# A four-layer graph network on one core: cycles of two packed groups and one scalar group, with TensorE's other work between the packed ones

## Chip, cores, metric

One Trainium2 chip, one of its cores. The metric is the device time of one execution in microseconds, the median of several runs.

## What is computed

Eight graphs (B = 8) of 2048 nodes with 128 features each and a dense 2048 x 2048 adjacency. Four layers, each with a residual and a normalisation of the rows:

```python
x = _layernorm(x + gnn0(x, adj))   # out = D^-1/2 (adj + I) D^-1/2 x, then @ W.T + b
x = _layernorm(x + attention(x))   # below
x = _layernorm(x + gnn2(x, adj))   # as layer 0 with |.| in the degrees
x = _layernorm(x + gnn3(x, adj))   # without I
```

```python
mask = jnp.where(adj > 0, 0.0, -1e22)
q, k = x @ WQ, x @ WK
h = relu(q[:, None, :, :] + k[:, :, None, :])     # 2048 x 2048 x 128 for each graph
att = softmax(einsum('bijd,d->bij', h, p) + mask)
out = att @ x
```

The attention makes the time: for each graph and each of its 2048 rows i, a relu over 128 x 2048 numbers and a product with p.

## The kernel before

The kernel writes out each engine's program by hand. The features lie on the 128 partitions. For one row i of the scores an engine makes one *row*, 128 x 2048: `relu(q + k_i)`, and TensorE multiplies it with a window of 32 columns in which one column is not zero, so that one of 32 partitions of `score` grows by it. Four rows, one in each quarter of the partitions, are a *group*; 32 groups (places g = 0 to 31) are a *block* of 128 rows i; 16 blocks are a *pass*, one graph's attention. There are 8 passes and 128 blocks, numbered here from 0; the first pass is blocks 0 to 15.

There are two kinds of groups. In a *scalar group* (kind "A") ScalarE makes the four rows in float32 (L908), and TensorE takes 16 matmuls, each in two records. In a *packed group* (kind "D") VectorE (L1088) and GpSimd (L688) make the rows as a maximum over pairs of half-precision numbers packed in a word; TensorE takes 32 matmuls, for the high and the low halves (L1247). `SCALAR_GROUPS` (L42) says which places are scalar, `makers` (L274) who makes each of the four rows: "DDPP" two by VectorE and two by GpSimd, "DPPP" one and three at the places of `THIRD_ROWS`, "AAAP" a scalar group with one row *lent* to GpSimd (`LENT_ROWS`). Rows lie in two rings, one for each kind, of two groups each (`RING = 2`): a row may be written when TensorE is done with the group two before it of the same kind (`rows_used`), and TensorE starts a group when all its rows are there (`rows_ready`).

Beside the scores of graph c+1, each pass does *side work* at fixed places: layers 2 and 3 of graph c, layer 0, queries and keys of graph c+2, each in four *steps* of one block (`BLOCK`: layer 2 in blocks 2 to 5 of the pass, layer 3 in 6 to 9, layer 0 in 10 to 13). A step on TensorE is 16 *pieces* of 128 x 512 (L1163, `PIECES_AT`), the self term (L1169), and a projection (L1181); ScalarE copies in between (`turn_layer`), VectorE sums and normalises (`SUM_AT`, `NORM_OUT_AT`), GpSimd adds the bias and takes roots. The adjacency of graph c+2 is transposed in 32 *units* of two halves, seven halves a block in the pass's blocks 0 to 8 (`SLOTS`, L1147); ScalarE copies each half out of one PSUM buffer `turn[1]` (`EVICT`, L808) and sums the unit's rows (`SUM_UNIT`, L818 and L821). Each block also does the softmax of the block before it: at place 1 VectorE reads the four banks of scores (`masked_scores`, L1040); group 0 of a block may write a bank only when it is read. Then ScalarE takes exponentials (`EXP_AT`, L880), TensorE transposes them (`TURN_AT`), ScalarE copies (`COPY_IN`, L884), TensorE multiplies (`MULTIPLY_AT`, L1224), VectorE normalises (`NORM_AT`) and makes the next mask (`MASK_AT`).

So four kinds of blocks: units only (21: blocks 0 to 8 of the first pass, 0 and 1 of the six middle ones), units and a step (42), a step only (42), and plain ones (23). In the two kinds with units, place 5 (`LEFT_OUT`) is a packed group instead of a scalar one: 11 scalar groups, and 12 in the others. An engine's program at a place is: the softmax's part, `side(c, place)`, then the group. Groups that follow each other on TensorE with no side work between them are shown by the trace as one run.

## Time and profile before

| | us |
|---|---|
| median of 3 runs (13930.92 to 13934.58) | 13932.96 |
| the profiled execution | 13921.96 |
| its span, first to last instruction | 13920.2 |
| TensorE busy | 12944.8 |
| ScalarE busy | 12465.2 |
| VectorE busy | 12353.1 |
| GpSimd busy | 11710.4 |

A chain of waits is followed back from the last instruction of a stretch, at each step to what released it. The profiled execution is 11.0 us under the median.

### The profile page before, as it was taken

How to read it: one execution, taken by the hardware profiler on the slowest of the kernel's cores; microseconds unless marked ns; L12 is line 12 of the kernel's file. 1: busy time of each engine (PE TensorE's matmuls, PEld its weight loads, DVE VectorE, ACT ScalarE, POOL GpSimd, SP SyncE). 2: the span in 40 equal slices, each digit the busy share in tenths (PEclk: the TensorE clock that was granted, in tenths of full speed). 3: DMA queues.
4: the chain of work that ended last, by engine and by line, in shares of the span. 5: the costliest groups of instructions: out<-in, count | busy, mean ns of one | idle time of the engine just before them, and what ended most of it. 6: DMA issues, size and time to landing. Idle time of an engine off the chain costs nothing.

```text
span 13920.2 us, 320252 instructions
## 1 busy us (share of the span) xinstructions
PE 12944.8 (93%) x143877; PEld 6304.3 (45%) x143877; DVE 12353.1 (89%) x8531; ACT 12465.2 (90%) x8292; POOL 11710.4 (84%) x6447
## 2 busy tenths in 40 slices
PE   7889989999899998999989999899998999999998
PEld 3444434444444444444444444444444444444443
DVE  6998998889988899888998889988899888998995
ACT  5999998899988999889998899988998889999994
POOL 4888888888888888888888888888888888888884
PEclk9999999999999999999999999999999999999999
DMA  4111112221122212222122211222112222111103
GB/s 143 52 46 48 52 57 82 86 64 48 61 82 89 61 43 65 85 88 61 38 74 82 87 57 45 68 85 84 56 45 73 82 83 62 36 47 56 43 16 110
DMA packets 752100, 918.85 MB, mean 66 GB/s; under 512 B 62608, under 2 KB 511120, under 8 KB 748688
## 3 DMA queue, kind: packets, MB, share of 16 engines
q1 hardware_dynamic: 750736, 898.36, 21.0%
q8 instruction: 1138, 18.64, 0.6%
q14 instruction: 226, 1.85, 0.0%
HBM read 705.23 MB, written 184.55 MB: 64 GB/s over the span
## 4 chain that ended last, share of the span: by engine, by line
PE 57%; ACT 18%; DVE 17%; POOL 6%; issue 2%; DMA 1%; SPq 0%; POOLq 0%; DVEq 0%; ACTq 0%
PE score L1247 42%; ACT scalar_rows L908 16%; DVE pair_rows L1088 15%; PE acc L1163 8%; POOL pair_rows L688 5%; PE turn L1134 3%; PE acc L1224 2%; PE acc L1181 1%; DVE q_pair L1016 0%; DMA piece<-adj_turned 0%; DVE gx L997 0%; PE acc L1169 0%; ACT q_pair L808 0%; PE turn L1193 0%; ACT att_turned L884 0%
## 5 line engine op out<-in xcount | busy, mean ns | idle before, releaser
L688 POOL TENSOR_SCALAR pair_rows<-q_pair,k_pair_cols 128x2050 f32<-128x2050 f32 x5628 | 11036.4, 1980 | 1855.6 <-PE score L1247 1827.5
L1088 DVE TENSOR_SCALAR pair_rows<-q_pair,k_pair_cols 128x2050 f32<-128x2050 f32 x4864 | 11076.7, 2341 | 1287.0 <-PE score L1247 1272.6
L908 ACT ACTIVATE scalar_rows<-q_f,k_cols 128x2048 f32<-128x2048 f32 x5808 | 11159.1, 2004 | 231.9 <-PE score L1247 222.0
L1247 PE MATMUL score<-pair_rows,unit_window 128*32 128x512 f16 x83936 | 5467.1, 396 | 713.7 <-DVE pair_rows L1088 560.6
L1247 PE MATMUL score<-scalar_rows,sign_window 128*32 128x512 f32 x46464 | 5424.5, 596 | 153.4 <-ACT scalar_rows L908 152.1
L1247 PEld LDWEIGHTS score<-pair_rows,unit_window 128*32 128x32 bf16 x83936 | 2873.8, 97 | 3452.7 <-issue 1043.0
L1247 PEld LDWEIGHTS score<-scalar_rows,sign_window 128*32 128x32 f32 x46464 | 1810.9, 110 | 2981.2 <-issue 2602.2
L1163 PE MATMUL acc<-piece,q_f 128*128 128x512 f32 x2944 | 1411.8, 602 | 17.0 <-DMA piece<-adj_turned 15.3
L808 ACT ACTIVATE q_pair<-turn 128x512 f32<-128x512 f32 x448 | 262.1, 585 | 765.5 <-PE turn L1134 765.5
L1163 PEld LDWEIGHTS acc<-piece,q_f 128*128 128x128 f32 x2944 | 502.6, 190 | 529.9 <-issue 469.1
L1224 PE MATMUL acc<-x,att_turned 128*128 128x128 f32 x4096 | 560.1, 280 | 0.0
L1224 PEld LDWEIGHTS acc<-x,att_turned 128*128 128x128 f32 x4096 | 505.6, 194 | 57.3 <-issue 57.3
L884 ACT ACTIVATE att_turned<-turn 128x512 f32<-128x512 f32 x512 | 301.4, 589 | 115.5 <-PE turn L1134 115.2
L1134 PEld LDWEIGHTS turn<-ident,att 128*128 128x128 f32 x2048 | 222.8, 145 | 321.4 <-issue 316.2
L1134 PE MATMUL turn<-ident,att 128*128 128x128 f32 x2048 | 347.9, 294 | 3.8 <-ACT att L880 3.1
L1040 DVE CUSTOM_DVE_ANT_0 att<-score,att 128x512 f32<-128x512 f32 x512 | 323.1, 685 | 11.7 <-PE score L1247 11.5
L1134 PE MATMUL turn<-ident,q_pair 128*128 128x128 f32 x1920 | 296.9, 279 | 27.7 <-DMA q_pair<-in_adj_dram 20.4
L1029 DVE TENSOR_SCALAR att<-att 128x2050 f32<-128x2050 f32 x128 | 291.7, 2279 | 0.0
L1134 PEld LDWEIGHTS turn<-ident,q_pair 128*128 128x128 f32 x1920 | 219.9, 142 | 122.3 <-issue 94.8
L880 ACT ACTIVATE att<-att,row_parts 128x2048 f32<-128x2048 f32 x128 | 256.4, 2003 | 12.9 <-DVE row_parts L1044 12.9
L821 ACT ACTIVATE y_turned<-q_pair 128x1024 bf16<-128x1024 f32 x224 | 237.0, 1058 | 7.1
L818 ACT ACTIVATE y_turned<-q_pair 128x1024 bf16<-128x1024 f32 x224 | 235.1, 1049 | 0.0
(101 smaller groups left out, 2664.9 us busy)
## 6 DMA issues: line engine op xcount, KB each, us to landing
piece<-adj_turned SPq DMA_DIRECT2D x1472, 256.0 KB, 2.8
q_pair<-in_adj_dram SPq DMA_DIRECT2D x240, 512.0 KB, 4.6
adj_turned<-q_pair SPq DMA_DIRECT2D x224, 512.0 KB, 4.9
att<-in_adj_dram SPq DMA_DIRECT2D x128, 820.0 KB, 4.9
att<-in_adj_dram SPq DMA_DIRECT2D x128, 204.0 KB, 5.1
q_f<-in_adj_dram SPq DMA_DIRECT2D x16, 512.0 KB, 5.5
gx<-in_x_dram SPq DMA_DIRECT2D x32, 256.0 KB, 3.9
adj_turned<-pair_rows SPq DMA_DIRECT2D x8, 1024.0 KB, 11.3
```

Of the source, the lines that this page charges most:

```text
L688: ins = pool.tensor_scalar(slot_row(n, g, u), pairs_of(c + 1), 3.0e38, k_pair_cols[:, t % 2, QUAD * u + g:QUAD * u + g + 1], ALU.min, ALU.max)
L808: nc.scalar.activation(stage(c)[:, k * BANK:(k + 1) * BANK], turn[1][:], ACT.Copy).then_inc(turn_free[1], 1)
L880: nc.scalar.activation(att, att, ACT.Exp, bias=neg_max, accum_out=row_sum).then_inc(exp_ready, 1)
L884: nc.scalar.activation(att_turned[:, cc % 2, :], turn[0][:], ACT.Copy).then_inc(turn_free[0], 1)
L908: ins = nc.scalar.activation(slot_row(n, g, u)[:, 0:N], q_of(c + 1), ACT.Relu, bias=k_cols[:, t % 2, QUAD * u + g:QUAD * u + g + 1])
L1029: nc.vector.tensor_scalar(att_wide[:, 0:N + 2], in_parts(att_wide), 0.0, NEG_INF, ALU.is_le, ALU.mult).then_inc(mask_ready, 1)
L1040: nc.vector.tensor_tensor_reduce(out=part, in0=score[:, cc, :], in1=part, scale=1.0, scalar=-3.0e38, op0=ALU.add, op1=ALU.max, accum_out=b ...
L1088: ins = nc.vector.tensor_scalar(slot_row(n, g, u), pairs_of(c + 1), k_pair_cols[:, t % 2, QUAD * u + g:QUAD * u + g + 1], None, ALU.max)
L1134: ins = nc.tensor.transpose(turn[k][:, j * P:(j + 1) * P], src(j), ident[:])
L1163: nc.tensor.matmul(acc[1][:], scaled(c)[:, i, :], turned, start=(i == 0), stop=(i == T - 1)) \
L1224: ins = nc.tensor.matmul(acc[0][:, 0:D], att_turned[:, cc % 2, j * P:(j + 1) * P], x1[:, cc * PER + j, :], start=(cc == 0 and j == 0), sto ...
L1247: ins = nc.tensor.matmul(score[QUAD * u:QUAD * (u + 1), cc, :], (unit_window if pair else sign_window)[:, QUAD - 1 - g:2 * QUAD - 1 - g], ...
```

## The change

Places are chosen anew. Scalar groups stand at every third place (2, 5, 8, ...) so that two packed groups and one scalar group follow each other; blocks with units or a step have eleven of them, plain ones twelve. Blocks of a step alone had twelve before. `PIECES_AT`, `SLOTS`, `TURN_AT` and `MULTIPLY_AT` put TensorE's side work at places 1, 4, 7, 10, ..., that is between the two packed groups, but for place 29. The steps' other places, those of the softmax and of queries and keys move with them, and GpSimd's extra rows (`THIRD_ROWS`, `LENT_ROWS`) too. On ScalarE, the exponentials and the copies of units, queries and keys go from ahead of a group's rows to the middle of them (`MID_ROW = 2`, the new function `copies`). `masked_scores` waits for the last group of the block, whatever its kind.

```diff
--- before.py
+++ after.py
@@ -38,14 +38,14 @@
     assert D == P and T % 2 == 0 and B > 2 and 2 * PER == T // 2
 
 
-    N_ACT = 12
-    SCALAR_GROUPS = [(a * GROUPS + GROUPS - 2) // N_ACT for a in range(N_ACT)]
-    LEFT_OUT = 5
+    SCALAR_GROUPS = {"steps": (2, 5, 8, 11, 14, 17, 20, 23, 26, 29, 31),
+                     "units": (2, 5, 8, 11, 14, 17, 20, 23, 26, 29, 31),
+                     "plain": (2, 5, 8, 11, 14, 17, 19, 22, 24, 27, 29, 31)}
     RING = 2
     PARTS = 5
     PART = (N + 2) // PARTS
     PITCH = PART + 2
-    assert PARTS % 2 == 1 and PART * PARTS == N + 2 and PART % 2 == 0 and LEFT_OUT in SCALAR_GROUPS
+    assert PARTS % 2 == 1 and PART * PARTS == N + 2 and PART % 2 == 0
 
     HALF = N // 2
     HALF_TILES = T // 2
@@ -57,17 +57,17 @@
 
 
     PLACES = T * GROUPS
-    SLOTS = [0, 6, 10, 14, 18, 23, 28]
-    EVICT = {0: 4, 6: 9, 10: 13, 14: 17, 18: 22, 23: 27, 28: 31}
-    SUM_UNIT = {0: 3, 6: 8, 10: 12, 14: 16, 18: 21, 23: 25, 28: 33}
+    SLOTS = [1, 4, 10, 19, 22, 25, 29]
+    EVICT = {1: 5, 4: 8, 10: 14, 19: 23, 22: 27, 25: 31, 29: 34}
+    SUM_UNIT = {1: 6, 4: 9, 10: 15, 19: 18, 22: 28, 25: 32, 29: 35}
     BLOCK = {"layer2": 2, "layer3": 6, "layer0": 10}
-    PIECES_AT = {-4: [0, 1, 2], 0: [3, 4, 5], 1: [6], 4: [7], 10: [8, 9], 14: [10], 18: [11], 23: [12, 13, 14, 15]}
-    SELF_AT, TURNED_AT, PROJECT_AT, SUM_AT, ROOT_AT, NORM_OUT_AT, STORE_AT = 18, 28, 28, 31, 33, 40, 41
-    SCALE_AT = {"layer2": [-25, -20, -15, -10], "layer3": [-5, -3, -1, 11], "layer0": [-5, -3, -1, 16]}
-    BIAS_AT, FIRST_LOAD_AT = 20, -8
-    QK = {"turn": 46, "copy": 49, "q": 50, "q_out": 54, "k": 55, "q_store": 56, "q_split": 58, "k_out": 59,
-          "q_high": 61, "k_store": 61, "q_pair_store": 62, "k_split": 76, "k_high": 78, "k_pair_store": 79}
-    X1_AT, X2_AT, X0_AT = 28, 34, 45
+    PIECES_AT = {-7: [0, 1, 2, 3], -3: [4, 5, 6, 7], 1: [8, 9], 4: [10], 7: [11], 13: [12], 16: [13], 19: [14, 15]}
+    SELF_AT, TURNED_AT, PROJECT_AT, SUM_AT, ROOT_AT, NORM_OUT_AT, STORE_AT = 16, 24, 22, 26, 28, 30, 31
+    SCALE_AT = {"layer2": [-25, -20, -15, -10], "layer3": [-8, -7, -6, 2], "layer0": [-8, -7, -6, 6]}
+    BIAS_AT, FIRST_LOAD_AT = 20, -12
+    QK = {"turn": 39, "copy": 43, "q": 42, "q_out": 46, "k": 45, "q_store": 48, "q_split": 49, "k_out": 49,
+          "q_high": 53, "k_store": 51, "q_pair_store": 54, "k_split": 56, "k_high": 60, "k_pair_store": 61}
+    X1_AT, X2_AT, X0_AT = 25, 30, 34
     DIAG_AT, DEGREE_AT, DIS_AT, KEEP_AT = 9 * GROUPS - 16, 9 * GROUPS + 8, 9 * GROUPS + 9, 11 * GROUPS + 9
 
     adj_turned = nc.dram_tensor("adj_turned", (B * STEPS * T, P, BANK), F32, kind="Internal").ap()
@@ -248,22 +248,28 @@
 
         block = ctx.enter_context(nc.Block())
 
-        TURN_AT = {6: 0, 10: 1, 14: 2, 18: 3}
-        COPY_IN = {10: 0, 13: 1, 18: 2, 23: 3}
-        MULTIPLY_AT = {10: 0, 14: 1, 18: 2, 23: 3}
-        MASK_AT, EXP_AT, NORM_AT, ATT_ROOT_AT, OUTPUT_AT = 24, 5, 27, 28, 31
-        MASK_LOAD_AT, K_LOAD_AT = 19, 21
+        TURN_AT = {4: 0, 7: 1, 10: 2, 13: 3}
+        COPY_IN = {8: 0, 11: 1, 14: 2, 17: 3}
+        MULTIPLY_AT = {7: 0, 10: 1, 13: 2, 16: 3}
+        MASK_AT, EXP_AT, NORM_AT, ATT_ROOT_AT, OUTPUT_AT = 22, 5, 20, 21, 24
+        MASK_LOAD_AT, K_LOAD_AT = 14, 21
+        MID_ROW = 2
 
         OPENING, FIRST, LAST, CLOSING = -2, -1, B - 2, B - 1
 
         MASKED_AT = (1, 1)
-        SPARE_AT = 9
-        THIN = (8, 9, 11, 12, 14)
-        THIRD_ROWS = {(True, True): (1, 25, 30), (True, False): (1, 25), (False, True): (1, 9, 25, 30), (False, False): (1, 25)}
-        LENT_ROWS = [(18, 3), (7, 3)]
+        ROOTS_BLOCK = 9
+        THIRD_ROWS = {"steps": (1, 3, 21, 25), "units": (1, 3, 21, 25), "roots": (1, 28), "plain": (1, 3, 21, 28)}
+        LENT_ROWS = [(11, 3), (23, 3)]
+
+        def sort_of(c, t):
+            if units_in(c, t) and t == ROOTS_BLOCK:
+                return "roots"
+            return "steps" if step_in(c, t) else "units" if units_in(c, t) else "plain"
 
         def kinds(c, t):
-            return ["A" if g in SCALAR_GROUPS and (g != LEFT_OUT or not units_in(c, t)) else "D" for g in range(GROUPS)]
+            groups = SCALAR_GROUPS[{"roots": "units"}.get(sort_of(c, t), sort_of(c, t))]
+            return ["A" if g in groups else "D" for g in range(GROUPS)]
 
         def units_in(c, t):
             return len(units_where(c, lambda u: slot_place(2 * u) // GROUPS == t)) > 0
@@ -273,11 +279,8 @@
 
         def makers(c, t, g):
             if kinds(c, t)[g] == "A":
-                lent = LENT_ROWS[:1 if step_in(c, t) else 2] if units_in(c, t) else []
-                return "".join("P" if (g, u) in lent else "A" for u in range(P // QUAD))
-            if units_in(c, t) and t == SPARE_AT and g in THIN:
-                return "DDDP"
-            return "DPPP" if g in THIRD_ROWS[units_in(c, t), step_in(c, t)] else "DDPP"
+                return "".join("P" if sort_of(c, t) == "units" and (g, u) in LENT_ROWS else "A" for u in range(P // QUAD))
+            return "DPPP" if g in THIRD_ROWS[sort_of(c, t)] else "DDPP"
 
         def one_of(c, *which):
             return c in which
@@ -410,7 +413,7 @@
             return c * 5 + 8
 
         def scored(n):
-            return groups_through(n - 1, SCALAR_GROUPS[-1]) + RING
+            return groups_through(n - 1, GROUPS - 1) + RING
 
         def flat(tiles):
             return tiles.rearrange("p t f -> p (t f)")
@@ -863,17 +866,19 @@
                         nc.scalar.activation(halves(pair_new(c))[:, :, 1], high(c), ACT.Copy, scale=(1.0, -1.0)[i]) \
                             .then_inc(high_written, 1)
 
-            def side(c, place):
+            def copies(c, place):
                 for k in range(2):
                     for u in units_where(c, lambda u: evict_place(2 * u + k) == place):
                         copy_unit(c, u, k)
+                queries_keys(c, place)
+
+            def side(c, place):
                 for u in units_where(c, lambda u: sum_place(u) == place):
                     sum_unit(c, u)
                 for name, s in steps_at(c, place, TURNED_AT):
                     turn_layer(c, name, s)
                 if place == DEGREE_AT and not one_of(c, LAST, CLOSING):
                     diag_sizes(c)
-                queries_keys(c, place)
 
             def exponentials(n):
                 act.wait_ge(neg_max_ready, n)
@@ -888,8 +893,6 @@
                     t, g = divmod(place, GROUPS)
                     before = t > 0 or not one_of(c, FIRST)
                     n = block_of(c, t)
-                    if before and g == EXP_AT:
-                        exponentials(n)
                     side(c, place)
                     if KINDS[n, g] == "A":
                         if first_made("A", n, g):
@@ -900,19 +903,24 @@
                                     act.wait_ge(piece_used, STEPS * T + AHEAD)
                             act.wait_ge(k_loaded[t % 2], (c + 1) * (T // 2 * 32) + (t // 2 * 32 + 32))
                         act.wait_ge(rows_used["A"], GROUP_NO[n, g] + 1)
-                        for u in range(P // QUAD):
-                            if before and u == 1 and g in COPY_IN:
+                    for u in range(P // QUAD):
+                        if u == MID_ROW:
+                            if before and g == EXP_AT:
+                                exponentials(n)
+                            if before and g in COPY_IN:
                                 copy_weights(c * T + (T + t - 1), COPY_IN[g])
-                            if MAKERS[n, g][u] != "A":
-                                continue
+                            copies(c, place)
+                        if MAKERS[n, g][u] == "A":
                             ins = nc.scalar.activation(slot_row(n, g, u)[:, 0:N], q_of(c + 1), ACT.Relu,
                                                        bias=k_cols[:, t % 2, QUAD * u + g:QUAD * u + g + 1])
+                    if KINDS[n, g] == "A":
                         ins.then_inc(rows_ready["A"], 1)
 
             for u in range(UNITS):
                 first_unit(u)
             for place in range(PLACES):
                 side(OPENING, place)
+                copies(OPENING, place)
             attention(FIRST)
             for c in range(B - 2):
                 attention(c)
@@ -922,6 +930,7 @@
                 copy_weights(B * T - 1, cc)
             for place in range(PLACES):
                 side(CLOSING, place)
+                copies(CLOSING, place)
 
 
         @block.vector
```

In the excerpts of the engines' programs, L1134, L1163, L1224, L1247 of before are L1143, L1172, L1233, L1256 of the change; on ScalarE L880, L884, L908, L808, L818, L821 are L885, L889, L914, L811, L821, L824.

TensorE, block 53 (block 5 of a middle pass, with units and a step): before, from the side work ahead of group 0 to the transposes around group 6. `x32` on pair rows is one packed group, `x64` two, `x16` on scalar rows one scalar group.

```order
L1134 MATMUL turn<-ident,q_pair 128x128 x4
L1163 MATMUL acc<-piece,q_f_0 128x512 x3
L1247 MATMUL score<-pair_rows,unit_window 32x512 x32
L1163 MATMUL acc<-piece,q_f_0 128x512
L1247 MATMUL score<-pair_rows,unit_window 32x512 x32
L1247 MATMUL score<-scalar_rows,sign_window 32x512 x16
L1247 MATMUL score<-pair_rows,unit_window 32x512 x32
L1163 MATMUL acc<-piece,q_f_0 128x512
L1247 MATMUL score<-pair_rows,unit_window 32x512 x64
L1134 MATMUL turn<-ident,att 128x128 x4
L1134 MATMUL turn<-ident,q_pair 128x128 x4
L1247 MATMUL score<-pair_rows,unit_window 32x512 x32
```

The same place of the change, from group 30 of the block before to group 4.

```order
L1256 MATMUL score<-pair_rows,unit_window 32x512 x32
L1256 MATMUL score<-scalar_rows,sign_window 32x512 x16
L1256 MATMUL score<-pair_rows,unit_window 32x512 x32
L1143 MATMUL turn<-ident,q_pair 128x128 x4
L1172 MATMUL acc<-piece,q_f_0 128x512 x2
L1256 MATMUL score<-pair_rows,unit_window 32x512 x32
L1256 MATMUL score<-scalar_rows,sign_window 32x512 x16
L1256 MATMUL score<-pair_rows,unit_window 32x512 x32
L1143 MATMUL turn<-ident,att 128x128 x4
L1143 MATMUL turn<-ident,q_pair 128x128 x4
L1172 MATMUL acc<-piece,q_f_0 128x512
L1256 MATMUL score<-pair_rows,unit_window 32x512 x32
```

Nothing stands between group 31 and group 0 any more; the side work stands after group 0 and after group 3, and the four packed groups 3 to 6 in a row are gone.

ScalarE in the same block, before: a unit's sums, group 2's rows, a unit's copy, the exponentials, group 7's rows (group 5 is packed), a sum and a copy, group 10's rows with a copy of weights after the first.

```order
L818 ACTIVATE y_turned,deg_part<-q_pair 128x1024
L821 ACTIVATE y_turned,abs_part<-q_pair 128x1024
L908 ACTIVATE scalar_rows<-q_f_1,k_cols 128x2048 x4
L808 ACTIVATE q_pair<-turn 128x512
L880 ACTIVATE att,row_parts<-att,row_parts 128x2048
L908 ACTIVATE scalar_rows<-q_f_1,k_cols 128x2048 x4
L818 ACTIVATE y_turned,deg_part<-q_pair 128x1024
L821 ACTIVATE y_turned,abs_part<-q_pair 128x1024
L808 ACTIVATE q_pair<-turn 128x512
L908 ACTIVATE scalar_rows<-q_f_1,k_cols 128x2048
L884 ACTIVATE att_turned<-turn 128x512
L908 ACTIVATE scalar_rows<-q_f_1,k_cols 128x2048 x3
```

The change: the last two rows of group 2, a sum, two rows of group 5, the exponentials and a copy, two rows of group 5 and two of group 8, two copies, two rows.

```order
L914 ACTIVATE scalar_rows<-q_f_1,k_cols 128x2048 x2
L821 ACTIVATE y_turned,deg_part<-q_pair 128x1024
L824 ACTIVATE y_turned,abs_part<-q_pair 128x1024
L914 ACTIVATE scalar_rows<-q_f_1,k_cols 128x2048 x2
L885 ACTIVATE att,row_parts<-att,row_parts 128x2048
L811 ACTIVATE q_pair<-turn 128x512
L914 ACTIVATE scalar_rows<-q_f_1,k_cols 128x2048 x4
L889 ACTIVATE att_turned<-turn 128x512
L811 ACTIVATE q_pair<-turn 128x512
L914 ACTIVATE scalar_rows<-q_f_1,k_cols 128x2048 x2
```

The exponentials and every copy now come after two of a scalar group's four rows.

## Rows read from the trace of the kernel before

**Rows 1.** The page: span, and busy time of each engine (share) xinstructions.

```profile
span 13920.2 us, 320252 instructions
...
PE 12944.8 (93%) x143877; PEld 6304.3 (45%) x143877; DVE 12353.1 (89%) x8531; ACT 12465.2 (90%) x8292; POOL 11710.4 (84%) x6447
```

**Rows 2.** Groups by line: shapes xcount | busy us, mean ns | idle before, releaser.

```profile
L1088 DVE TENSOR_SCALAR pair_rows<-q_pair,k_pair_cols 128x2050 f32<-128x2050 f32 x4864 | 11076.7, 2341 | 1287.0 <-PE score L1247 1272.6 <-DMA q_pair<-q_pair_kept 11.8
L688 POOL TENSOR_SCALAR pair_rows<-q_pair,k_pair_cols 128x2050 f32<-128x2050 f32 x5628 | 11036.4, 1980 | 1855.6 <-PE score L1247 1827.5 <-DMA q_pair<-q_pair_kept 24.9
```

**Rows 3.** Stretches of equal blocks: length, busy (x) by engine, PEclk, DMA share, GB/s.

```profile
194.00:1129.20 935.20, 808.76 (x9852) 381.90 (x9852) 873.08 (x487) 844.16 (x615) 820.80 (x433) 0.98 0.16 49
...
5293.20:5395.80 102.60, 89.09 (x1106) 41.74 (x1108) 97.20 (x56) 92.43 (x71) 92.63 (x50) 1.00 0.17 55
5395.80:5505.00 109.20, 95.76 (x1115) 44.27 (x1114) 98.11 (x60) 99.75 (x71) 94.85 (x53) 0.98 0.27 78
5505.00:6279.70 774.70, 732.38 (x8013) 366.95 (x8012) 685.62 (x486) 680.53 (x499) 656.43 (x361) 0.99 0.28 85
6279.70:6392.20 112.50, 103.86 (x1117) 51.31 (x1120) 91.54 (x67) 97.59 (x60) 99.73 (x62) 0.97 0.19 59
6392.20:6810.10 417.90, 410.60 (x4495) 206.29 (x4495) 372.80 (x272) 391.11 (x234) 359.54 (x198) 1.00 0.19 57
6810.10:7010.30 200.20, 180.82 (x2157) 82.99 (x2158) 194.38 (x119) 192.86 (x114) 168.47 (x90) 0.97 0.10 34
...
13170.30:13739.90 569.60, 526.08 (x6432) 237.65 (x6432) 549.10 (x323) 563.37 (x321) 492.63 (x263) 0.99 0.05 15
```

**Rows 4.** Chain of waits by engine and line: 5505.0 to 6279.7, then 194.0 to 1129.2.

```profile
by line: PE score L1247 53.1%; DVE pair_rows L1088 24.6%; PE acc L1163 10.3%; PE turn L1134 4.3%; PE acc L1224 3.4%; ACT scalar_rows L908 1.9%; DVE gx L997 1.0%; PE acc L1181 0.8%; PE acc L1169 0.5%; issue 0.2%; ACT y_turned L818 0.1%; ACT 
by line: ACT scalar_rows L908 53.2%; DVE pair_rows L1088 26.2%; PE score L1247 7.7%; issue 4.8%; ACT q_pair L808 2.5%; ACT y_turned L818 1.6%; PE turn L1134 1.5%; ACT att_turned L884 1.2%; ACT y_turned L821 0.8%; PE acc L1224 0.8%; ACTq L81
```

**Rows 5.** Chain of waits in block 53, in order of time: start us, us.

```profile
5839.03 18.14 DVE pair_rows L1088 x8
...
5915.13 3.44 PE acc L1163 x8
```

**Rows 6.** Timeline of TensorE, groups 1 to 4 of block 53: start us, us.

```profile
5839.97 2.02 PE L1247 MATMUL score<-pair_rows,unit_window 128*32 128x512 f16 x32
5841.79 3.64 PE L1247 MATMUL score<-scalar_rows,sign_window 128*32 128x512 f32 x32
5845.22 2.07 PE L1247 MATMUL score<-pair_rows,unit_window 128*32 128x512 f16 x32
5847.22 1.12 PE L1163 MATMUL acc<-piece,q_f 128*128 128x512 f32 x2
5848.27 2.04 PE L1247 MATMUL score<-pair_rows,unit_window 128*32 128x512 f16 x32
```

**Rows 7.** Timeline of TensorE, group 9 of block 53, and its stretch as in Rows 3.

```profile
5867.53 3.60 PE L1247 MATMUL score<-pair_rows,unit_window 128*32 128x512 f16 x32 [2.45 <-DVE pair_rows L1088]
...
5867.50:5871.10 3.60, 3.57 (x33) 1.12 (x33) 3.60 (x2) 0.00 (x0) 1.60 (x1) 0.53 0.00 0
```

**Rows 8.** Timeline of ScalarE in block 53, groups 5 to 10: start us, us [idle before].

```profile
5838.07 1.99 ACT L880 ACTIVATE att<-att,row_parts 128x2048 f32<-128x2048 f32 x1
...
5840.05 7.71 ACT L908 ACTIVATE scalar_rows<-q_f,k_cols 128x2048 f32<-128x2048 f32 x4
5847.64 1.06 ACT L818 ACTIVATE y_turned<-q_pair 128x1024 bf16<-128x1024 f32 x1
...
5857.36 0.60 ACT L808 ACTIVATE q_pair<-turn 128x512 f32<-128x512 f32 x1 [7.38 <-PE turn L1134]
```

**Rows 9.** Timeline of TensorE around the start of block 46.

```profile
5088.03 3.68 PE L1247 MATMUL score<-scalar_rows,sign_window 128*32 128x512 f32 x32
5092.99 2.39 PE L1247 MATMUL score<-pair_rows,unit_window 128*32 128x512 f16 x32 [1.28 <-DVE bank_max L1040]
5097.32 0.87 PE L1247 MATMUL score<-pair_rows,unit_window 128*32 128x512 f16 x12 [1.95 <-POOL pair_rows L688]
```

## The prediction, made before the change was run

> **What bounds the kernel now.** I read the page's busy line first. TensorE is busy 93% of the span, ScalarE 90%, VectorE 89%, GpSimd 84% [rows 1]; the clocks of the four make no clear bottleneck, and TensorE's idle 13920.2 - 12944.8 = 975 us is what any better order could win back, a little more if the clock rises with it. The groups by line show 4864 rows of VectorE and 5628 of GpSimd (and 84 lent ones), and that both wait for TensorE to free a row buffer, 1273 and 1828 us [rows 2]. So they wait for each other in turn, through rings of two groups.
>
> Next, the time by stretches of equal blocks [rows 3], where I divide by the number of blocks. In a middle pass (six of the eight) block 0 has units only and takes 102.6 us, block 1 109.2, blocks 2 to 8 (units and a step) 774.7/7 = 110.7, block 9 112.5, blocks 10 to 13 (a step) 417.9/4 = 104.5, blocks 14 and 15 100.1. The first pass has nine unit blocks of 935.2/9 = 103.9, the last pass ends with six plain ones of 569.6/6 = 94.9. In a step block TensorE is busy 410.6 of 417.9 us: it is the bound there. In the blocks of 110.7 us it is idle 42 of 775 us, and no other engine is above 98 of 110.7.
>
> The chain of waits says why [rows 4]: in blocks 2 to 8 VectorE's pair rows hold 24.6% of it and gx 1.0%, which is 198 of 774.7 us or 28.3 a block; in the first pass's unit blocks ScalarE's rows hold 53.2% and VectorE's 26.2%. Block 53 (pass 2, block 5) shows the place: one run of VectorE from 5839.03 until TensorE starts group 9 at 5867.53, for groups 3 to 9 [rows 5, 7]. Four packed groups stand in a row there (3, 4, 5, 6), and VectorE's two rows of each take 18.14/8 x 2 = 4.54 us, where TensorE needs 1.8.
>
> **Prices on TensorE**, start to start [rows 6]: a packed group 5841.79 - 5839.97 = 1.82, a scalar group 3.43, a packed group before other work 2.00, one piece between packed groups 1.05. Two matmul records of a piece cost 0.86 (3.44/8 x 2, [rows 5]). So a break in the score matmuls costs 0.18 going out and 1.05 - 0.86 = 0.19 coming back, at most 0.37; where the next group is scalar it is less. From group 1 to the start of group 9 TensorE took 27.56 us (5867.53 - 5839.97, rows 6 and [rows 7]) for work of 1.82 + 3.43 + 2.00 + 1.05 + 1.82 + 2.00 + 1.03 (two transposes with their break, like the piece) + 1.82 + 3.43 + 1.82 = 20.2: 7.3 lost. Group 9 then lasts 3.5 instead of 2.0, because the granted clock of that stretch is 0.53, so mostly the lower level of 1.2 GHz, after a pause of 2.45 us [rows 7]. That makes 8.9 a block, and 110.7 - 8.9 = 101.8 is TensorE's own work in such a block.
>
> **The change in loads.** Counted from the tables over all 128 blocks:
> - ScalarE 5808 to 5682 rows, -126 x 1.93 (7.71/4, [rows 8]) = -243 us. All of it is in step blocks, 48 to 44 rows; blocks 2 to 8 get one row more, 43 to 44.
> - VectorE 4864 to 4818, -46 x 2.27 = -104: two rows less in unit-only and plain blocks, one less in blocks 2 to 8, two more in step blocks.
> - GpSimd 5712 to 5884, +172 x 1.98 [rows 2] = +341, two rows more everywhere but in blocks 2 to 8.
> - TensorE: 42 scalar groups become packed, 42 x (1.82 - 3.43) = -68; 42 of the scalar groups no longer have a lent row, which lets them run full length, between 0 and +0.4 each, taken as +16; the breaks between score matmuls and other work rise from 1021 to 1152 in the program's order, 131 x 0.28 (between 0.19 and 0.37) = +37. Together about -15. Its own work hardly moves, so what is won must come from waits.
>
> The breaks are the one thing that speaks against the change in kind. The Trainium skill (TensorEngine Tiling (Array Packing), Key Properties) says that changing the tiling mode drains TensorE. If a drain cost a whole matmul's 0.6 us twice, the breaks would be +157 instead of +37 and 13,600; the rows show 0.37 at most.
>
> **Blocks 2 to 8, 42 of them.** The DDA cycles now cost TensorE 1.82 + 2.00 + 0.19 + 3.43 = 7.4 plus some 2.2 of other work, 9.6; VectorE needs 4 x 2.27 = 9.1 (6.8 where GpSimd makes three), GpSimd 7.9, ScalarE 7.7 plus copies. I walked VectorE through a block: rows of a packed group may start once the group two before is done, about 2.1 after that one's start. Its rows are ready 2 us early nearly everywhere, 0.4 early at group 28. At the block's start group 1 has one VectorE row only; it ends about 0.9 us before the scalar group 31 does, so the banks are being read when TensorE comes to group 0. So the 8.9 us go. What comes new:
> - The transpose of a unit at place 29 needs the buffer that ScalarE empties in the middle of group 31's rows. Those start when scalar group 26 is done, 3.7 after its start; two rows and a copy (3.85 + 0.6) make 8.1, TensorE is there after 3.43 + 1.82 + 2.00 = 7.25: 0.9 late, in every unit block.
> - The exponentials stand in the middle of group 5's rows, TensorE's first transpose of them at place 4. Group 2's rows start when scalar group 29 is done, 8.7 - 3.7 = 5.0 before group 0 starts; four rows and a copy (8.3), two rows (3.85) and the exponentials (2.0) end 9.2 after it [rows 8]. TensorE is there after 2.00 + 2.2 + 0.2 + 1.82 + 3.43 + 2.00 = 11.7. Where a sum precedes (5847.64 to 5857.36 - 7.38 = 2.3 us, [rows 8]) only 0.2 is left: 0.3 lost on average.
> - Projecting at place 22 needs a copy that ScalarE makes at 24, after group 23's rows: 0.3.
> I take 101.8 + 0.4 (no lent row) + 0.3 (one break more) + 1.5 = 104.0; 110.7 - 104.0 = 6.7, x 42 = **-281**. Ends: 0, and -8.9 x 42 = -374.
>
> **Unit-only blocks, 21.** There the busiest engine is ScalarE with 844.2/9 = 93.8, VectorE 97.0, GpSimd 91.2 in 103.9 us [rows 3]; after, VectorE 97.0 - 4.5 = 92.5, GpSimd 91.2 + 4.0 = 95.2. ScalarE waits there for transposes (7.38 us before one copy in block 53, [rows 8]); its copies now stand mid-group, a cycle or more behind the transpose. Halfway between 103.9 and 95.2: -4.4 x 9. Block 0 of a middle pass -3.1 x 6; block 1, which the DDA order helps too, -6.2 x 6, where GpSimd, 94.9 + 4, is next. Sum **-95**; ends 0 and -190.
>
> **Step blocks, 36 without block 9.** TensorE is the bound: -1.6 for the scalar group, +0.3 for the breaks. VectorE rises from 372.8/4 = 93.2 to 97.7, still under TensorE's 102.65 - 1.3 = 101.3, so the idle 7.3/4 = 1.8 stays: -1.3 x 36 = **-47**. Ends: +20 (the VectorE rows bind) and -1.3 - 1.8 each, -112.
>
> **Block 9 of the middle passes, 6.** The table "roots" asks for units and block 9, and no unit starts in block 9 (the 64th slot is the second half of one that starts in block 8). So this part does nothing: the block gets the rows of "steps", GpSimd 99.7 + 4.0 = 103.7 in 112.5. Taken as **0**; ends -20 and +25.
>
> **Plain blocks, 23.** 12 scalar groups as before; ScalarE is the bound of the last pass's (563.4/6 = 93.9 busy of 94.9): 0. Blocks 14 and 15 lose two VectorE rows and block 15 the queries' and keys' work: -2 x 15 = **-30**; ends 0 and -50.
>
> The opening and the closing (194 us before the first block, 180 after the last) keep their order: 0, within 10.
>
> Sum: -281 - 95 - 47 + 0 - 30 = **-453**. The profiled execution took 13921.96 (its span 13920.2), 11.0 under the median of the three runs; 13932.96 - 453 = 13480, so **13,480 us**, 3.3% less.
>
> **The rivals.**
> 1. *Fewer waits, but not most of them.* The rings stay two groups deep, and VectorE's 9.1 against TensorE's 9.6 leaves 0.5 us a cycle: each sum, norm or mask (2 to 4 us) on VectorE takes several cycles to make up. For it: the sums and norms did keep VectorE on the chain for 24.6% there, though TensorE had pauses to share. Half of the 453 stays: 13,706.
> 2. *The waits only move.* The VectorE run goes from groups 3 to 9 into every cycle and the time stays within 28 us, 0.2%, about what a measurement of this kernel can tell from no change.
> 3. *Slower: the start of a block.* Before, blocks with units or a step had a transpose, three pieces or both between group 31 and group 0, which hid VectorE's reading of the banks. Now nothing stands there. Block 46, which had nothing there either, shows the price: group 31 starts at 5088.03, group 0 at 5092.99, 1.5 over 3.43, then 2.5 over 1.82 until group 1 at 5097.32 [rows 9], 4.0 in all. In 105 blocks that is +424, and with VectorE late into groups 3 to 9 only half the gain comes, -227: 14,130. It decides if VectorE ends group 1's row after group 31; in block 46 GpSimd's three rows were late as well. Against it: the piece and transpose at place 1 and the single VectorE rows at groups 1 and 3.
> 4. *More than I say:* unit blocks reach their busiest engine and step blocks lose all idle time, 453 + 200 (the ends of unit-only and step blocks, 95 + 65, and 40 of blocks 2 to 8): 13,280.
>
> **How the numbers follow.** Forecast (from 13,350 to 13,620) 0.55, rival 4 0.15, rival 1 0.18, rival 2 0.04, rival 3 0.08. The ends of the terms add to -374 - 190 - 112 - 20 - 50 = -746 and +45, unlikely together. Range 13,260 to 13,740 leaves out rivals 2 and 3 and a rest. Faster 0.55 + 0.15 + 0.18 = 0.88, same 0.04, slower 0.08.
>
> **What would show it.** Blocks 2 to 8 at about 104 us, no wait of over 2 us for VectorE before group 5, 6 or 9, VectorE's share of their chain under 15%; the granted clock of these blocks near 1.00; TensorE idle about 530 us in all; a new wait of the unit transpose for ScalarE's copy, about 0.9 us in 63 blocks. Block 9 unchanged. I am wrong if group 0 starts late in most blocks, or if the chain of blocks 2 to 8 still has VectorE at a fifth.

## The result, and the profile after

13,566 us, median of four runs (13,555 to 13,572), against 13,932 for the kernel before on the same chip: ratio 0.9737, 95% interval 0.972 to 0.9754. That is -366 us where -453 was forecast. The forecast of 13,480 was 86 us too low, inside its range. In the profiled executions the span fell from 13,920.2 [rows 1] to 13,565.4, by 354.8. One of the four executions of `f3_roots_block`, below, took 28,219 us at a granted clock of 0.43 and is left out.

The page of the kernel after: the busy line, and the groups of the row makers (columns as in rows 2).

```profile
span 13565.4 us, 320252 instructions
...
PE 12859.9 (95%) x143877; PEld 6172.4 (46%) x143877; DVE 12293.0 (91%) x8485; ACT 12236.5 (90%) x8166; POOL 12073.6 (89%) x6619
...
L691 POOL TENSOR_SCALAR pair_rows<-q_pair,k_pair_cols 128x2050 f32<-128x2050 f32 x5842 | 11478.0, 1986 | 1158.8 <-PE score L1256 1123.7
L1097 DVE TENSOR_SCALAR pair_rows<-q_pair,k_pair_cols 128x2050 f32<-128x2050 f32 x4818 | 11010.7, 2341 | 953.9 <-PE score L1256 931.1
```

TensorE is idle 13,565.4 - 12,859.9 = 705 us, not 975 as before and not the 530 of the forecast. GpSimd's and VectorE's waits for a free row buffer fell from 1828 and 1273 us [rows 2] to 1124 and 931.

The stretches of equal blocks after, in the form of rows 3: the nine unit blocks of the first pass; block 0, block 1, blocks 2 to 8, block 9, blocks 10 to 13 and blocks 14 and 15 of a middle pass; the six last plain ones.

```profile
199.50:1092.50 893.00, 811.43 (x9852) 391.02 (x9852) 831.58 (x467) 845.52 (x612) 854.79 (x450) 0.99 0.17 51
5140.80:5239.70 98.90, 89.44 (x1104) 43.51 (x1097) 91.69 (x52) 94.76 (x69) 92.64 (x50) 1.00 0.22 67
5239.70:5343.00 103.30, 96.46 (x1121) 46.32 (x1121) 92.67 (x54) 95.84 (x72) 98.49 (x55) 1.00 0.26 80
5343.00:6079.60 736.60, 726.98 (x8018) 347.53 (x8017) 673.88 (x484) 692.82 (x503) 658.14 (x362) 1.00 0.30 90
...
6079.60:6190.10 110.50, 101.59 (x1120) 46.57 (x1119) 96.21 (x70) 91.80 (x59) 106.32 (x65) 1.00 0.20 60
...
6190.10:6610.70 420.60, 405.74 (x4496) 190.59 (x4493) 398.28 (x289) 364.58 (x221) 378.73 (x208) 1.00 0.18 54
6610.70:6806.80 196.10, 179.09 (x2155) 85.00 (x2157) 181.85 (x110) 192.45 (x113) 176.68 (x93) 0.98 0.10 33
...
12809.30:13380.90 571.60, 525.02 (x6432) 251.67 (x6432) 522.25 (x307) 563.75 (x321) 513.78 (x273) 0.99 0.05 14
```

Divided by the number of blocks and set against [rows 3]: unit-only 103.9 to 99.2, block 0 102.6 to 98.9, block 1 109.2 to 103.3; blocks 2 to 8 110.7 to 736.60/7 = 105.2, with TensorE idle 10 us in place of 42; block 9 112.5 to 110.5; **blocks 10 to 13 up**, 417.9 to 420.6, with VectorE busy 398 in place of 373. There TensorE's busy time fell from 410.6 to 405.7 as forecast, but its idle time rose from 7.3 to 14.9. Taken so over all 128 blocks from the starts of their groups:

| kind of block | forecast | measured |
|---|---|---|
| units and a step, 42 | -281 | -236 |
| units only, 21 | -95 | -103 |
| a step, 36 without block 9 | -47 | +23 |
| block 9 of middle passes, 6 | 0 | -10 |
| plain, 23 | -30 | -39 |
| opening and closing | 0 | +10 |
| sum | -453 | -355 |

The chain of waits by line, kernel after: blocks 2 to 8, blocks 10 to 13, block 9.

```profile
by line: PE score L1256 54.4%; ACT scalar_rows L914 13.2%; PE acc L1172 11.1%; PE turn L1143 4.7%; POOL pair_rows L691 4.0%; PE acc L1233 3.1%; DMA adj_turned<-q_pair 2.1%; issue 2.1%; ACT y_turned L824 0.9%; ACT y_turned L821 0.8%; PE acc 
...
by line: PE score L1256 42.5%; DVE pair_rows L1097 24.9%; PE acc L1172 7.1%; POOL pair_rows L691 6.5%; issue 4.9%; PE acc L1233 2.8%; PE turn L1143 2.5%; DVE q_pair L1025 1.9%; DVE q_pair L1019 1.2%; PE turn L1202 1.2%; DVE att L1038 0.9%; 
...
by line: POOL pair_rows L691 69.4%; PE score L1256 9.8%; POOL dis_new L741 7.3%; issue 4.4%; PE acc L1172 3.3%; POOL q_f L722 2.7%; POOL gx L729 1.1%; POOL rstd L670 0.9%; POOL row_parts L676 0.5%; POOL deg_sum L706 0.2%; POOL var_eps L668 
```

In blocks 2 to 8 VectorE's quarter [rows 4] is gone from the first places; a quarter of VectorE now stands in blocks 10 to 13 instead, and GpSimd holds block 9.

### The profile page after: what moved, and what is told of

Same layout as the page of the kernel before. It is cut to its first block, busy times and chain, and to the rows that moved or that the text cites. A ratio compares the mean times of both kernels' runs of the same rounds, so it can differ in the third digit from the quotient of the medians.

```text
span 13565.4 us, 320252 instructions
## 1 busy us (share of the span) xinstructions
PE 12859.9 (95%) x143877; PEld 6172.4 (46%) x143877; DVE 12293.0 (91%) x8485; ACT 12236.5 (90%) x8166; POOL 12073.6 (89%) x6619
## 4 chain that ended last, share of the span: by engine, by line
PE 53%; ACT 19%; POOL 14%; DVE 9%; issue 3%; DMA 1%; SPq 0%; POOLq 0%; ACTq 0%; DVEq 0%
PE score L1256 39%; ACT scalar_rows L914 16%; POOL pair_rows L691 12%; PE acc L1172 7%; DVE pair_rows L1097 7%; PE turn L1143 3%; PE acc L1233 2%; DVE q_pair L1025 1%; ACT att L885 1%; DMA adj_turned<-q_pair 1%; ACT y_turned L824 1%; ACT q_pair L811 1%; ACT y_turned L821 1%; POOL dis_new L741 0%; DMA piece<-adj_turned 0%
## 5 line engine op out<-in xcount | busy, mean ns | idle before, releaser
L691 POOL TENSOR_SCALAR pair_rows<-q_pair,k_pair_cols 128x2050 f32<-128x2050 f32 x5842 | 11478.0, 1986 | 1158.8 <-PE score L1256 1123.7
L914 ACT ACTIVATE scalar_rows<-q_f,k_cols 128x2048 f32<-128x2048 f32 x5682 | 10941.8, 2001 | 997.6 <-PE score L1256 989.2
L1256 PE MATMUL score<-pair_rows,unit_window 128*32 128x512 f16 x85280 | 5567.6, 394 | 474.2 <-POOL pair_rows L691 278.2
L1256 PE MATMUL score<-scalar_rows,sign_window 128*32 128x512 f32 x45456 | 5251.1, 595 | 81.7 <-ACT scalar_rows L914 80.2
L1256 PEld LDWEIGHTS score<-pair_rows,unit_window 128*32 128x32 bf16 x85280 | 2779.8, 96 | 3489.6 <-issue 1603.9
L1256 PEld LDWEIGHTS score<-scalar_rows,sign_window 128*32 128x32 f32 x45456 | 1784.9, 110 | 2748.5 <-issue 2350.0
L1172 PE MATMUL acc<-piece,q_f 128*128 128x512 f32 x2944 | 1408.8, 601 | 19.7 <-DMA piece<-adj_turned 18.6
L1172 PEld LDWEIGHTS acc<-piece,q_f 128*128 128x128 f32 x2944 | 504.4, 191 | 495.9 <-issue 433.0
L1233 PE MATMUL acc<-x,att_turned 128*128 128x128 f32 x4096 | 554.9, 279 | 0.0
L1233 PEld LDWEIGHTS acc<-x,att_turned 128*128 128x128 f32 x4096 | 498.4, 192 | 57.4 <-issue 57.4
L1143 PE MATMUL turn<-ident,att 128*128 128x128 f32 x2048 | 337.3, 287 | 30.3 <-ACT att_turned L889 21.7
L1143 PE MATMUL turn<-ident,q_pair 128*128 128x128 f32 x1920 | 306.8, 284 | 34.9 <-ACT q_pair L811 24.5
L1143 PEld LDWEIGHTS turn<-ident,att 128*128 128x128 f32 x2048 | 215.8, 141 | 264.4 <-issue 190.1
L889 ACT ACTIVATE att_turned<-turn 128x512 f32<-128x512 f32 x512 | 298.2, 582 | 5.3 <-PE turn L1143 5.3
L1143 PEld LDWEIGHTS turn<-ident,q_pair 128*128 128x128 f32 x1920 | 208.9, 141 | 191.9 <-issue 154.8
L811 ACT ACTIVATE q_pair<-turn 128x512 f32<-128x512 f32 x448 | 261.2, 583 | 31.0 <-DMA adj_turned<-q_pair 29.4
L885 ACT ACTIVATE att<-att,row_parts 128x2048 f32<-128x2048 f32 x128 | 255.4, 1995 | 6.4 <-DVE row_parts L1053 6.4
L824 ACT ACTIVATE y_turned<-q_pair 128x1024 bf16<-128x1024 f32 x224 | 237.2, 1059 | 7.1
L821 ACT ACTIVATE y_turned<-q_pair 128x1024 bf16<-128x1024 f32 x224 | 235.6, 1052 | 0.0
```

Source lines behind the costliest of these rows:

```text
L691: ins = pool.tensor_scalar(slot_row(n, g, u), pairs_of(c + 1), 3.0e38, k_pair_cols[:, t % 2, QUAD * u + g:QUAD * u + g + 1], ALU.min, ALU.max)
L811: nc.scalar.activation(stage(c)[:, k * BANK:(k + 1) * BANK], turn[1][:], ACT.Copy).then_inc(turn_free[1], 1)
L821: nc.scalar.activation(unread, raw(c), ACT.Copy, accum_out=deg_part[:, u % 2, u // 2:u // 2 + 1]).then_inc(raw_summed, 1)
L824: nc.scalar.activation(unread, raw(c), ACT.Abs, accum_out=abs_part[:, u % 2, u // 2:u // 2 + 1]).then_inc(raw_abs_summed, 1)
L885: nc.scalar.activation(att, att, ACT.Exp, bias=neg_max, accum_out=row_sum).then_inc(exp_ready, 1)
L914: ins = nc.scalar.activation(slot_row(n, g, u)[:, 0:N], q_of(c + 1), ACT.Relu, bias=k_cols[:, t % 2, QUAD * u + g:QUAD * u + g + 1])
```

## Experiments

### Either half alone

`e1_groups_alone` is the kernel before with the tables of groups (and the copies of weights also in packed groups); `e2_places_alone` is the change with those tables put back, so the new order within ScalarE's groups belongs to its half.

```diff
-    N_ACT = 12
-    SCALAR_GROUPS = [(a * GROUPS + GROUPS - 2) // N_ACT for a in range(N_ACT)]
+    SCALAR_GROUPS = {"steps": (2, 5, 8, 11, 14, 17, 20, 23, 26, 29, 31),
...
+        THIRD_ROWS = {"steps": (1, 3, 21, 25), "units": (1, 3, 21, 25), "roots": (1, 28), "plain": (1, 3, 21, 28)}
+        LENT_ROWS = [(11, 3), (23, 3)]
```

> The kernel before with the new scalar groups, makers and lent rows alone; all side work, softmax places and copies stand as before (where a copy of weights stood inside a scalar group that is now packed, it is made at the same place ahead of the next rows). Theory G (the groups make the gain: four packed groups in a row are gone, so VectorE no longer holds TensorE): blocks 2 to 8 of a middle pass fall from 110.7 to 106 or less, the whole to 13,650-13,750 us. Rival P (the place of the side work makes it: between two packed groups it gives VectorE its time): blocks 2 to 8 stay over 108.5, the whole at 13,800-13,930 us.

> The changed kernel with the old scalar groups, makers and lent rows: four packed groups 3 to 6 in a row in blocks with units, side work at the new places 1, 4, 7, 10, ... Theory G: VectorE's run over groups 3 to 9 stays, blocks 2 to 8 at 109-111 us, the whole at 13,830-13,950 us. Rival P: blocks 2 to 8 at 106 or less, the whole at 13,650-13,750 us. If both this and the groups alone stay over 13,800, it takes both together.

Groups alone: 13,992, ratio 1.0044 (1.0029 to 1.0059). Places alone: 13,950, ratio 1.0015 (1.0005 to 1.0025). So neither part brings the gain, and each alone costs something; together they bring 2.6%. Both theories missed the time of the first; the second came out as theory G had it (109 to 111 a block). Blocks 2 to 8 of the two, as in rows 3, and for the second the wait that is left there (us in total, times, longest):

```profile
5534.20:6286.90 752.70, 726.47 (x8013) 365.68 (x8012) 669.47 (x477) 694.86 (x506) 657.75 (x361) 1.00 0.29 87
```

```profile
5493.10:6256.90 763.80, 730.18 (x8018) 345.30 (x8013) 687.31 (x491) 682.16 (x496) 656.92 (x362) 1.00 0.29 87
...
PE score L1254 <- DVE pair_rows L1095: 27.7, 21, 2.5
```

107.5 and 109.1 a block: more than half of the 110.7 - 105.2 comes from the groups there. What the first loses is in its step blocks: blocks 12 and 13 of this pass take 111 or more each. That the extra GpSimd rows at 21 and 25 meet norms and splits at their old places there is the likely reason; no run separates it.

### Order within ScalarE, and the twelfth scalar group

`e3_copies_ahead`: `MID_ROW = 2` becomes `0`, so exponentials and copies come ahead of the four rows. `e4_twelve_in_steps`: blocks with a step and no unit keep twelve scalar groups.

> The changed kernel with MID_ROW = 0: exponentials and all copies stand ahead of a group's rows again, two rows earlier on ScalarE. Theory M (mid-group copies matter since ScalarE would otherwise wait for TensorE's transposes before it can make rows): unit-only blocks rise from 99.2 to 101-103 us and the whole to 13,610-13,680 us. Rival N (they do not matter; earlier copies even end the wait of the transpose at place 29 for its buffer, 0.55 us in 63 blocks): 13,520-13,570 us.

> The changed kernel with twelve scalar groups again in blocks that have a step and no unit (places and makers of plain blocks): VectorE 36 instead of 38 rows there, GpSimd 44 instead of 46, ScalarE 48 instead of 44. Theory V (step blocks did not gain because VectorE and GpSimd got two rows more each, beside the queries' and keys' splits): blocks 10 to 13 of a middle pass fall from 105.2 to 102-104 us, block 9 from 110.8 to 108 or less, the whole to 13,490-13,550 us. Rival T (TensorE is their bound, as forecast, and a scalar group costs it 1.6 more): blocks 10 to 13 rise to 106-107, the whole to 13,590-13,640 us.

Copies ahead: 13,691, 0.9831 (0.9817 to 0.9846), 124 us of the gain given back, more than either theory had. Blocks 2 to 8 take 756.8/7 = 108.1, and 2.9 x 42 = 122 is nearly all of it; unit-only ones did not rise to 101 as theory M had it. ScalarE in block 53 shows how, then TensorE there:

```profile
5717.20 7.70 ACT L914 ACTIVATE scalar_rows<-q_f,k_cols 128x2048 f32<-128x2048 f32 x4
5724.78 0.59 ACT L889 ACTIVATE att_turned<-turn 128x512 f32<-128x512 f32 x1
5726.61 0.60 ACT L811 ACTIVATE q_pair<-turn 128x512 f32<-128x512 f32 x1 [1.23 <-DMA adj_turned<-q_pair]
...
5721.84 2.05 PE L1256 MATMUL score<-pair_rows,unit_window 128*32 128x512 f16 x32
5724.95 3.65 PE L1256 MATMUL score<-scalar_rows,sign_window 128*32 128x512 f32 x32 [1.05 <-ACT scalar_rows L914]
```

The four rows of group 5 come behind the exponentials and a copy, and TensorE starts 3.1 after the group ahead instead of 1.8; the next copy waits for the store of the one before, and the next group's rows wait behind it.

Twelve in steps: 13,593, 0.976 (0.9745 to 0.9774). Blocks 10 to 13 take 106.9 on average, 1.7 more, about what a scalar group costs over a packed one (rival T), so eleven are right there. Block 9 takes 107.5 with it, 3 us less: that block has too much for GpSimd.

### What holds blocks 11 to 13

In a middle pass only the blocks behind a step of layer 0 got longer: block 10 went from 103.6 to 102.5, as forecast, but 11 and 12 from 105.6 to 106.4 and 13 from 103.1 to 105.3. They make the queries and keys. A *split* is two instructions of VectorE on 128x512, a bitwise and (L1019) and a subtraction (L1025). The split of q stands at place 17, that of k at place 24. VectorE in block 59 (block 11) after, then GpSimd at the one of q and, from 6359.80, at the one of k:

```profile
6342.14 0.41 DVE L1019 TENSOR_SCALAR q_pair<-q_pair 128x512 int32<-128x512 int32 x1
6342.59 0.75 DVE L1025 TENSOR_TENSOR q_pair<-q_pair 128x512 f16<-128x512 f32 x1
6343.22 9.11 DVE L1097 TENSOR_SCALAR pair_rows<-q_pair,k_pair_cols 128x2050 f32<-128x2050 f32 x4
...
6362.53 1.47 DVE L1019 TENSOR_SCALAR q_pair<-q_pair 128x512 int32<-128x512 int32 x1
6364.04 2.45 DVE L1025 TENSOR_TENSOR q_pair<-q_pair 128x512 f16<-128x512 f32 x1
6366.38 6.84 DVE L1097 TENSOR_SCALAR pair_rows<-q_pair,k_pair_cols 128x2050 f32<-128x2050 f32 x3
...
6337.68 3.92 POOL L691 TENSOR_SCALAR pair_rows<-q_pair,k_pair_cols 128x2050 f32<-128x2050 f32 x2 [1.23 <-PE score L1256]
6342.96 4.14 POOL L691 TENSOR_SCALAR pair_rows<-q_pair,k_pair_cols 128x2050 f32<-128x2050 f32 x2 [1.35 <-PE score L1256]
...
6359.80 18.26 POOL L691 TENSOR_SCALAR pair_rows<-q_pair,k_pair_cols 128x2050 f32<-128x2050 f32 x9
```

The same two instructions take 0.41 + 0.75 us where GpSimd is idle (6341.6 to 6343.0) and 1.47 + 2.45 beside its rows. Before the change the split of q, at place 26, took 0.54 + 0.78 (block 59, first two lines), since GpSimd's run of rows ended there; that of k, at place 12 of the next block, stood beside seven rows of GpSimd and took 0.42 + 2.43 (block 60, last three lines):

```profile
6572.42 0.54 DVE L1010 TENSOR_SCALAR q_pair<-q_pair 128x512 int32<-128x512 int32 x1
6572.99 0.78 DVE L1016 TENSOR_TENSOR q_pair<-q_pair 128x512 f16<-128x512 f32 x1
...
6630.36 0.42 DVE L1010 TENSOR_SCALAR q_pair<-q_pair 128x512 int32<-128x512 int32 x1
6630.81 2.43 DVE L1016 TENSOR_TENSOR q_pair<-q_pair 128x512 f16<-128x512 f32 x1
...
6620.62 14.42 POOL L688 TENSOR_SCALAR pair_rows<-q_pair,k_pair_cols 128x2050 f32<-128x2050 f32 x7 [1.18 <-PE score L1247]
```

So the split of k was dear before too, 2.85, and is 3.92 now; that of q went from 1.32 to 1.16. The change moved the one of k from place 76 to 56 counted from its step, one block earlier: blocks 11 and 12, which had three splits of 5.5 us in all, have four of 10.2. It now stands in GpSimd's run of nine rows, just ahead of group 24. TensorE waits there (after, block 59; the last line is the stretch from the end of group 18 to group 28, in the form of rows 3):

```profile
6365.70 3.65 PE L1256 MATMUL score<-scalar_rows,sign_window 128*32 128x512 f32 x32
6371.02 2.04 PE L1256 MATMUL score<-pair_rows,unit_window 128*32 128x512 f16 x32 [1.66 <-DVE pair_rows L1097]
...
6384.65 1.58 PE L1256 MATMUL score<-pair_rows,unit_window 128*32 128x512 f16 x24 [0.69 <-DVE pair_rows L1097]
...
6352.90:6384.70 31.80, 28.77 (x315) 13.09 (x316) 31.66 (x29) 25.03 (x16) 30.78 (x20) 1.00 0.26 73
```

5.32 start to start instead of 3.43. In that stretch VectorE is busy 31.66 of 31.80 us, GpSimd 30.78, TensorE 28.77. Three runs asked whether the split's place, VectorE's load or the place of its single rows can take the wait away.

```diff
-          "q_high": 53, "k_store": 51, "q_pair_store": 54, "k_split": 56, "k_high": 60, "k_pair_store": 61}
+          "q_high": 53, "k_store": 51, "q_pair_store": 54, "k_split": 63, "k_high": 66, "k_pair_store": 67}
```

> The changed kernel with the split of the keys on VectorE moved from place 24 of a block to place 31 (k_split 56 to 63, k_high 60 to 66, the store 61 to 67). Theory K (in blocks 10 to 13 VectorE has norm, mask, output, split and sum within places 20 to 26, and the split alone, 3.9 us in block 59, makes TensorE wait before groups 24 and 28, 2.8 us there): these blocks fall from 105.2 to about 102.5-103.5 us, the whole to 13,500-13,530 us. Rival L (the debt only moves to the start of the next block, where VectorE reads the banks): within 13,550-13,585 us.

13,570, ratio 0.9737 (0.9721 to 0.9753): nothing, as rival L had it, and blocks 11 and 12 take 106.4 again. The split still stands beside GpSimd's rows (1.67 + 2.41 at 6391.78), the wait before group 24 is gone, and one of 1.4 for the reading of the banks stands before the next block's group 0.

`g1_row_at_18` and `g2_row_at_24` give blocks 11 to 13 a table of their own, `(1, 3, 18, 21, 25)` and `(1, 3, 21, 24)` in place of `(1, 3, 21, 25)`.

> Edit of the changed kernel: in the blocks 11 to 13 that have a step (21 blocks in seven passes) a fifth packed group, 18, gets three rows of GpSimd and one of VectorE. Those blocks take 106.5, 106.4 and 105.5 us in a middle pass of the changed kernel, and TensorE waits 1.9 us for VectorE before group 24 there. Theory W (VectorE has too much work in those blocks): a row of 2.3 us less takes that wait away in 21 blocks, -35 to -45 us, 13,520 to 13,530. Theory P (the wait belongs to the place): at group 21 VectorE waits for a free row buffer anyway (its rows start at 6353.27, 0.9 us after TensorE is through with group 19), so what it saves at 18 is lost again before the splits at 24: within 8 us of the changed kernel, 13,560 to 13,574, and the wait before group 24 stays at 1.6 to 2.

> Edit of the changed kernel: in the blocks 11 to 13 that have a step the single VectorE row stands at group 24 instead of 25; no engine gets more or fewer rows. Theory P (the wait belongs to the place): the splits end at 6366.4 and one row is ready 2.3 us later, at 6368.7, before TensorE is there at 6369.1; so the 1.9 us before group 24 go, VectorE's two rows of group 25 are ready in time, and part comes back at groups 27 and 28: -1.5 to -2.3 us in 21 blocks, -31 to -48, 13,518 to 13,535. Theory W (too much work for VectorE): nothing changes in the sum, the wait of 1.9 us turns up before group 25 or 27; 13,560 to 13,574.

Row at 18: 13,555, 0.9731 (0.9718 to 0.9745), at the edge of the changed kernel's own scatter; row at 24: 13,565, 0.9737 (0.9724 to 0.975). Blocks 11 and 12 take 106.3 and 106.6, as before; the wait changes its place and owner. First row at 18, then row at 24:

```profile
6361.97 2.04 PE L1258 MATMUL score<-pair_rows,unit_window 128*32 128x512 f16 x32 [1.83 <-POOL pair_rows L693]
6363.80 3.65 PE L1258 MATMUL score<-scalar_rows,sign_window 128*32 128x512 f32 x32
6367.23 2.06 PE L1258 MATMUL score<-pair_rows,unit_window 128*32 128x512 f16 x32
...
6381.39 2.04 PE L1258 MATMUL score<-pair_rows,unit_window 128*32 128x512 f16 x32 [1.23 <-POOL pair_rows L693]
```

```profile
6373.73 2.04 PE L1258 MATMUL score<-pair_rows,unit_window 128*32 128x512 f16 x32 [1.03 <-POOL pair_rows L693]
...
6388.01 2.04 PE L1258 MATMUL score<-pair_rows,unit_window 128*32 128x512 f16 x32 [1.30 <-DVE pair_rows L1099]
```

Theory P falls with it: with the single row at 24 it had -31 to -48, and with the row at 18 a wait before group 24 that is gone. Theory W missed the first run (-35 to -45) and had the time of the second. What fits these kernels is the sum of VectorE's work between two points. It can't start group 21's row before TensorE is through with group 18 (a ring of two; 6352.9 in the changed kernel, not 0.9 us after group 19, as I had written), and from there, 6353.27, it works without a pause until 6384.60, when group 28 is ready: 10 rows x 2.27 (groups 21, 22, 24, 25, 27, 28), the mask 2.2, the split 3.85, the output and the sum 2.6 make 31.35 of the 31.33, against TensorE's own 28.8. A row saved at 18 lies ahead of that stretch (there GpSimd, with a row more at 18, also comes late for groups 22 and 28), one moved from 25 to 24 stays in it, and a split put behind it falls due in the next. This account is inferred from the traces and not shown by a run: what would cut the stretch, a further GpSimd row between 22 and 28, was not run. GpSimd has little to spare there, since TensorE already waits 0.68 for its rows of group 22.

### Block 9, a unit's copy, the scalings

One line each: `f3_roots_block` lets the table "roots" apply in block 9 of the six middle passes, `f4_copy_at_30` copies the unit of place 25 at 30, not 31, `f5_scale_spread` spreads a layer's scalings on GpSimd.

```diff
-            if units_in(c, t) and t == ROOTS_BLOCK:
+            if t == ROOTS_BLOCK and step_in(c, t) and not one_of(c, LAST):
-    EVICT = {1: 5, 4: 8, 10: 14, 19: 23, 22: 27, 25: 31, 29: 34}
+    EVICT = {1: 5, 4: 8, 10: 14, 19: 23, 22: 27, 25: 30, 29: 34}
-    SCALE_AT = {"layer2": [-25, -20, -15, -10], "layer3": [-8, -7, -6, 2], "layer0": [-8, -7, -6, 6]}
+    SCALE_AT = {"layer2": [-25, -20, -15, -10], "layer3": [-8, -4, 0, 2], "layer0": [-8, -4, 0, 6]}
```

> The changed kernel with the table for block 9 made to apply (extra GpSimd rows at places 1 and 28 alone, where block 9 now takes 1, 3, 21, 25 as every step block): 12 rows go from GpSimd to VectorE in all. Theory R (GpSimd bounds block 9, 106.3 busy of 110.5 us): block 9 falls by 3 to 4 us, 18 to 24 in all, 13,540-13,550 us. Rival S (VectorE, 96 + 4.6 us, or the order binds at once): block 9 falls by less than 1 us, 13,560-13,575.

> The changed kernel with the copy of the half unit of place 25 at place 30, ahead of scalar group 31's rows, instead of in their middle. Theory B (the buffer is what TensorE's transpose at place 29 waits for, 0.55 us in 42 and 0.4 in 21 blocks): that wait is gone, 13,535-13,548 us. Rival C (the copy is off the path, since GpSimd's rows of group 28 or the next group bind at once): 13,558-13,572 us.

> The changed kernel with GpSimd's scaling of nodes for layers 3 and 0 spread over places -8, -4, 0 instead of -8, -7, -6 of the layer's first block. Theory Z (three scalings, 3.1 us, within places 24 to 26, and the root at 28 make GpSimd late for groups 25 and 28 in block 5, which takes 108.0 us where its neighbours take 104.7): block 5 falls to 105-106 us and block 9 by about 1, 13,535-13,552 us. Rival Y (block 5's 3 us are something else): block 5 stays at 107-108, 13,560-13,572 us.

13,545 (0.972, 0.9704 to 0.9736), 13,541 (0.972, 0.9705 to 0.9734) and 13,548 (0.9725, 0.9711 to 0.974): -21, -25 and -18. These are the times of theories R, B and Z. Each interval overlaps that of the change; the blocks say more. Block 9 with its table (110.5 before this edit), and blocks 2 to 8 with the copy at 30 (736.60 before it):

```profile
6072.50:6181.00 108.50, 102.81 (x1122) 47.38 (x1121) 100.57 (x72) 91.91 (x59) 102.54 (x63) 0.98 0.21 61
```

```profile
5333.10:6065.10 732.00, 726.09 (x8018) 351.09 (x8018) 673.75 (x484) 692.97 (x503) 658.10 (x362) 1.00 0.31 90
```

With the copy at 30 the line "PE turn L1143 <- ACT q_pair L811", 24.5 us in 53 waits of the whole changed kernel, is gone from this stretch. Block 9 fell by 2.0 in the pass shown, less than the 3 to 4 of theory R. The scalings act on block 5, where three of them stood among GpSimd's rows of groups 22 to 27 and TensorE then waited before group 28 (after, block 53: GpSimd, then TensorE):

```profile
5728.02 1.07 POOL L722 TENSOR_TENSOR q_f<-gx,dis_use 128x512 f32<-128x512 f32 x1
5729.05 3.96 POOL L691 TENSOR_SCALAR pair_rows<-q_pair,k_pair_cols 128x2050 f32<-128x2050 f32 x2
5732.94 1.07 POOL L722 TENSOR_TENSOR q_f<-gx,dis_use 128x512 f32<-128x512 f32 x1
5733.96 5.91 POOL L691 TENSOR_SCALAR pair_rows<-q_pair,k_pair_cols 128x2050 f32<-128x2050 f32 x3
5739.80 1.07 POOL L722 TENSOR_TENSOR q_f<-gx,dis_use 128x512 f32<-128x512 f32 x1
...
5750.20 3.07 PE L1256 MATMUL score<-pair_rows,unit_window 128*32 128x512 f16 x32 [2.86 <-POOL pair_rows L691]
```

Spread out, block 5 of the last pass falls from 107.0 to 104.4, of the middle ones from 108.0 to 106.8 on average, less than theory Z's 105 to 106. In block 53 of that run TensorE still waits for GpSimd before group 28:

```profile
5747.78 3.60 PE L1256 MATMUL score<-pair_rows,unit_window 128*32 128x512 f16 x32 [2.23 <-POOL pair_rows L691]
```

### Together

> The three edits that gained 21, 25 and 18 us one by one, together: block 9 gets the rows of the table for it, a unit's copy stands at place 30 instead of 31, the scalings of a layer are spread over places -8, -4, 0 instead of -8, -7, -6. By blocks they gained at different places (block 9; blocks 1 to 8; block 5), but some 6 us of each were in blocks 14 and 15, the same ones each time, which can only be won once. Theory A (independent but for those): 13,566 - 64 + 12 = 13,514, within 8. Theory S (they pay the same debt of the row makers): no more than the best of them, 13,535 to 13,545.

> The three edits together (13,512) and two more: the fifth packed group with three GpSimd rows (18) in blocks 11 to 13, and GpSimd's adding of the bias at place 12 instead of 20. Alone the fifth one gained 11 us: TensorE's waits before groups 24 and 27 became shorter by 3 us in block 13, and new ones of 1.1 and 0.2 for GpSimd stood before groups 22 and 21. Theory G (both row makers are full from group 18 to 28, and what is taken out of that stretch is won): GpSimd adds the bias (1.3 us) between groups 18 and 21, and waits 0.4 to 1.4 us per cycle for a free buffer between groups 12 and 18; with the bias at 12 its rows for 21 and 22 come 1.3 us earlier, so some 1 us more is won in 21 blocks: 13,512 - 11 - 21 = 13,480, within 10, and blocks 11 and 12 fall from 106.4 to about 105. Theory H (the bias there costs nothing, since the rows of group 21 wait for their buffer anyway): 13,501, within 6, blocks 11 and 12 stay at 106.4.

Three edits: **13,512** (13,510 to 13,514), ratio 0.9699 (0.9686 to 0.9712), 54 us under the change: they add up, less the 12 us that they share, as theory A had it to 2 us. Five edits, with the row at 18 and the bias at 12: 13,517 (13,508 to 13,522), 0.9703 (0.9689 to 0.9716), no different. Blocks 11 and 12 still take 212.7 together. Theory H was nearer, but its 13,501 within 6 missed too: the 11 us of the row at 18 did not come again. With the bias out of the way GpSimd is no later than in the change, and TensorE's waits in block 59 are those of the change: 0.67 before group 22, 1.68 before 24, 0.66 before 28. VectorE works from 6323.10 to 6354.45 there, 31.35 us, as the sum above has it, though it had waited 2.1 us for a buffer before group 19.

```profile
6262.50:6475.20 212.70, 206.66 (x2262) 97.30 (x2258) 197.28 (x145) 183.11 (x113) 192.57 (x106) 1.00 0.21 63
```

## Why the prediction was right, and where it was wrong

- **Blocks 2 to 8.** The mechanism held: the run of VectorE from group 3 to 9 is gone, its share is under 15%, the granted clock is 1.00. The gain was put 45 us too large, 104.0 a block against 105.2. The copy at 31 is not what was lacking: the sum had the wait for it at 0.9 a block. The transpose's wait measured 24.5/53 = 0.5, and moving the copy won 0.7 a block in the pass shown (736.60 - 732.00 over 7), 0.4 over all unit blocks (25 us over 63). What no step of the sum spoke of is the collision on GpSimd in block 5, which takes 108.0 where its neighbours take 104.7, 0.5 a block over the seven; the scalings hold 1.2 of those 3.3. The rest of the 1.2 a block stays open.
- **Unit-only and plain blocks.** -103 and -39 for -95 and -30. The unit-only term, halfway to the busiest engine, was right within 10%, but it was a guess without a mechanism, and no run here shows why it is half: luck.
- **Group 0 on time.** In block 59 it starts 3.43 after group 31 and lasts 2.26, 0.3 over. In blocks 2 to 8 no wait of TensorE for the reading of the banks is over 0.5 us, so rival 3 is refuted (in the whole kernel TensorE's matmuls wait 11.2 us for it, in 8 waits):

```profile
6289.14 3.67 PE L1256 MATMUL score<-scalar_rows,sign_window 128*32 128x512 f32 x32
6292.57 2.34 PE L1256 MATMUL score<-pair_rows,unit_window 128*32 128x512 f16 x32
6294.83 1.98 PE L1172 MATMUL acc<-piece,q_f 128*128 128x512 f32 x4
```

- **Step blocks: the step that failed.** The step was that VectorE "rises from 372.8/4 = 93.2 to 97.7, still under TensorE's 102.65 - 1.3 = 101.3, so the idle 7.3/4 = 1.8 stays": -47 forecast, +23 measured. TensorE's busy time fell as forecast, but its idle time doubled, from 7.3 to 14.9 us in blocks 10 to 13. Three errors are in it. I averaged over blocks 10 to 13, while VectorE is busy 96.1 in block 10 and 201.6/2 = 100.8 in 11 and 12, as much as TensorE had in the forecast. I costed the moved splits at nothing: blocks 10 to 13 hold six in place of five, and each one of k takes 3.9 in place of 2.85, so that they take 15.3 us in place of 9.6; this is most of what VectorE rose (25.5 us) beyond its rows (8 x 2.27 = 18.2). And a mean says nothing of a stretch of 31 us in which VectorE has no pause. The upper end I gave that term, +20 if "the VectorE rows bind", is about what came.
- **Block 9.** That the table "roots" never applies was right, and the run in which it applies shows what it is for: 2.0 us in the block shown. Block 9 came out at -10 for 0; no run says why.
- **Breaks on TensorE.** Its busy time fell by 85 us, not by 15; part of that is clock (0.987 to 0.992 over the span, 0.5% or some 65 us by my estimate). A drain of 0.6 us at each side of every break is not in these rows: group 0 and the pieces behind it above take 2.26 and 1.92 (until 6296.75), where the forecast's own prices give 2.00 and 2 x 0.86 + 0.19 = 1.91.
- **Opening and closing.** +10, at the bound given.

The sum is off by 98 of 453: +45 and +70, with -8, -9, -10 and +10 beside them. What each half does alone was not part of the forecast, and would have been missed: I would have given the groups most of the gain.

## To carry over

When a schedule is moved, sum each engine's work between two points it can't cross, from where a ring frees the buffer to where the rows fall due; a block's mean hides it. Move the new order of groups and the places of the other work together: either alone cost 0.2 to 0.4% here and both won 2.6%. Ask of small VectorE operations like those of a split what GpSimd does beside them.

## What the hardware showed unexpectedly

The two VectorE instructions of a split, a bitwise and (L1019) and a subtraction (L1025) on 128x512, took 0.41 + 0.75 us with GpSimd idle and 1.47 + 2.45 beside its rows of 1.97 us, 1.1 and 1.7 more, each less than one row; VectorE's long rows took 2.3 throughout. The Trainium skill (SBUF — State Buffer, Who interferes with whom) says that a VectorE instruction with two SBUF inputs contends with a GpSimd instruction that reads SBUF, and calls the port pair that they share an exclusive lock. The subtraction fits that: before and after the change, each of the 56 that started while a row of GpSimd was under way ended 0.62 to 0.65 us after that row, and each of the 72 others took 0.73 to 0.80.

The bitwise and has one SBUF input, and it is held too. In the changed kernel 28 of its 64 executions started while a row of GpSimd was under way; they took 1.45 to 1.55 us and each ended 0.28 us after that row. The 36 others took 0.41 to 0.43. GpSimd pays as well: its two rows from 6363.7 on, which met the two instructions, took 2.15 and 2.46 us. So what decides is whether GpSimd is in the middle of a row. Why this instruction contends, and the long rows of the same kind do not, stays open; it is the faster one, 0.41 us for 512 numbers a partition against 2.3 for 2050.
